# Attention after a group norm: the weighted sum of values by key tile in four PSUM banks, the projections in the banks of the scores

## The reference

```
x:   32 images of 32 x 32 places with 256 channels, float32
n  = group norm of x per image (32 groups of 8 channels, eps 1e-5)
q, k, v = n Wq + bq, n Wk + bk, n Wv + bv          (1024 tokens x 256)
attn    = softmax(q k^T / 16) over the keys
out     = x + (attn v) Wo + bo
```

## Time and profile before

| | us |
|---|---|
| median of three runs (lowest, highest) | 1810.69 (1810.49, 1810.78) |
| the profiled execution, its own time | 1810.44 |
| its span, first to last instruction | 1808.7 |
| PE busy in it | 1800.0 |
| DVE busy | 1662.2 |
| ACT busy | 985.4 |

### The profile page before, as it was taken

The page is one execution under the profiler, slowest core; times in us unless marked ns, Lnnn a source line. Parts: engine busy times, 40 slices in busy tenths (PEclk is TensorE's granted clock), DMA queues, the critical chain, the costliest instruction groups (busy, mean ns, idle before and its releaser), DMA issues.

```text
span 1808.7 us, 32719 instructions
## 1 busy us (share of the span) xinstructions
PE 1800.0 (100%) x11589; PEld 1643.6 (91%) x11589; DVE 1662.2 (92%) x2924; ACT 985.4 (54%) x1352; POOL 91.2 (5%) x106
## 2 busy tenths in 40 slices
PE   9999999999999999999999999999999999999999
PEld 8989999899998998999999989999899898999989
DVE  7999999999999999999999999999999999999997
ACT  4564554655645546556465564554654645646553
POOL 0000000000000000000000000000000000000000
PEclk9999999999999999999999999999999999999999
DMA  3221122221223202223122221122220222212201
GB/s 117 59 70 43 39 70 58 70 62 20 70 58 70 69 13 69 61 66 70 36 46 70 58 70 51 30 70 58 70 67 14 70 58 70 70 22 59 67 14 36
DMA packets 28808, 101.92 MB, mean 56 GB/s; under 512 B 3189, under 2 KB 3962, under 8 KB 28794
## 3 DMA queue, kind: packets, MB, share of 16 engines
q0 software_dynamic: 9072, 33.03, 11.7%
q1 hardware_dynamic: 19722, 68.69, 11.6%
HBM read 68.16 MB, written 66.58 MB: 74 GB/s over the span
## 4 chain that ended last, share of the span: by engine, by line
PE 96%; DVE 2%; issue 1%; ACT 1%; DMA 0%; POOL 0%; SPq 0%; DVEq 0%; POOLq 0%
PE ps_s L832 47%; PE ps_o L920 13%; PE ps_o L922 13%; PE ps_o L921 13%; PE ps_o L832 10%; DVE top L577 0%; DMA s_buf<-in_L_conv_Wk_dram 0%; DVE s_buf L607 0%; ACT s_buf L349 0%; ACT p_hi L343 0%; DVE o_buf L627 0%; DVE bn_parts L482 0%; DVE h_lo L550 0%; POOL group_stats L292 0%; ACT s_buf L335 0%
## 5 line engine op out<-in xcount | busy, mean ns | idle before, releaser
L920 PE MATMUL ps_o<-v_rows,p_hi 128*128 128x258 f32 x2048 | 581.5, 284 | 0.0
L922 PE MATMUL ps_o<-v_rows,p_lo 128*128 128x258 f32 x2048 | 576.4, 281 | 0.0
L921 PE MATMUL ps_o<-v_lo,p_hi 128*128 128x256 f32 x2048 | 574.4, 280 | 0.0
L343 ACT ACTIVATE p_hi<-s_buf 128x1024 fp32r<-128x1024 f32 x256 | 272.0, 1063 | 506.4 <-DVE s_buf L607 506.4
L832 PE MATMUL ps_s<-g_hi,h_hi 128*128 128x512 f32 x1024 | 399.3, 390 | 1.5 <-DVE v_lo L563 1.4
L832 PE MATMUL ps_s<-g_hi,h_lo 128*128 128x512 f32 x1024 | 399.0, 390 | 0.0
L832 PE MATMUL ps_s<-g_lo,h_hi 128*128 128x512 f32 x1024 | 398.8, 389 | 0.0
L921 PEld LDWEIGHTS ps_o<-v_lo,p_hi 128*128 128x128 f32 x2048 | 388.9, 190 | 2.9
L920 PEld LDWEIGHTS ps_o<-v_rows,p_hi 128*128 128x128 f32 x2048 | 385.8, 188 | 2.4
L922 PEld LDWEIGHTS ps_o<-v_rows,p_lo 128*128 128x128 f32 x2048 | 387.4, 189 | 0.0
L335 ACT ACTIVATE s_buf<-ps_s 128x512 f32<-128x512 f32 x512 | 292.8, 606 | 160.3 <-PE ps_s L832 158.8
(11 more groups left out here) (95 smaller groups left out, 2197.3 us busy)
## 6 DMA issues: line engine op xcount, KB each, us to landing
x_t<-in_x_turned_dram SPq DMA_DIRECT2D x64, 512.0 KB, 3.9
out_dram<-in_x_dram SPq DMA_DIRECT2D x63, 512.0 KB, 7.6
out_dram<-o_buf POOLq DMA_DIRECT2D x63, 512.0 KB, 5.5
x_last<-in_x_dram SPq DMA_DIRECT2D x1, 512.0 KB, 8.2
out_dram<-o_buf SPq DMA_DIRECT2D x4, 128.0 KB, 2.1
s_buf<-in_L_conv_Wq_dram SPq DMA_DIRECT2D x1, 256.0 KB, 5.0
s_buf<-in_L_conv_Wk_dram SPq DMA_DIRECT2D x1, 256.0 KB, 5.3
s_buf<-in_L_conv_Wv_dram SPq DMA_DIRECT2D x1, 256.0 KB, 5.5
```

Source lines behind the costliest of these rows:

```text
L343: nc.scalar.activation(p_hi[c][:, rows, :], s_buf[c][:, rows, :], ACT.Exp, scale=SCALE).then_inc(p_hi_done, 1)
L920: nc.tensor.matmul(ps[:, 0:VC], p_hi[c][:, m, cols], v_hi[:, m, :], start=m == 0, stop=False)
L921: nc.tensor.matmul(ps[:, 0:C], p_hi[c][:, m, cols], v_lo[:, m, :], start=False, stop=False)
L922: last = nc.tensor.matmul(ps[:, 0:VC], p_lo[c][:, m, cols], v_hi[:, m, :], start=False, stop=m == T - 1)
```

## The change

The attend loops over the key tiles outside and the four query tiles inside (`weigh`, `keys_ready`, `attend`), so that the four banks of `ps_o` are open at once and a piece of `p_lo` and `v_lo` is waited for when its key tile comes. The last attend of all keeps the old loop order (`attend_last`). The projections of g and v use the four banks of `ps_s`; the constants' banks are swapped in return. `scores` therefore waits for a g or v low part at each of its first four key tiles, and `project_v` for the scores of the chunk before it, bank by bank. DVE gets new orders: in the loop all finishes stand later (finish 0 after the stats, 1 behind project 0, 2 and 3 between the p_rests), and in the last image the four differences and the four finishes of (30, 1) stand ahead of the v_rests. ACT changes in the first image (order of v) and in the last (v parts between the exps). Left out of the diff are the two orders of the first image: there the v_rests stand between part maxima, query maxima, row maxima and the first two differences, in the order 0 to 3, and the four finishes of (0, 0) between the last p_rests of (0, 1).

```
...
         ps_s = banks("ps_s", SB)
         ps_o = banks("ps_o", TQ)
-        ps_g = [ps_o[0], ps_o[1], ps_s[2], ps_s[3]]
-        ps_turn = [ps_o[0], ps_o[1], ps_s[2]]
-        ps_a, ps_vo, ps_gb, ps_ob, ps_idle = ps_s[0], ps_s[1], ps_s[3], ps_o[3], ps_o[2]
+        ps_g = ps_s
+        ps_turn = [ps_s[0], ps_s[1], ps_s[2]]
+        ps_a, ps_vo, ps_gb, ps_ob, ps_idle = ps_o[0], ps_o[1], ps_o[2], ps_o[3], ps_s[3]
         ident = sb("ident", [P, P])
...
-        FIRST_V = (2, 3, 0, 1)
...
                 nc.scalar.activation(g_hi[:, k, c * Q:(c + 1) * Q], ps_g[i][:], ACT.Identity,
                                      bias=g_bias[:, k:k + 1]).then_inc(g_hi_done, 1)
-            def v_part(b, i, nth=None):
-                act.wait_ge(v_ps, b * 4 + (i if nth is None else nth) + 1)
+            def v_part(b, i):
+                act.wait_ge(v_ps, b * 4 + (i + 1))
                 nc.scalar.activation(v_hi[:, 2 * i:2 * i + 2, 0:C], ps_g[i][:].rearrange("p (t n) -> p t n", t=2),
                                      ACT.Copy).then_inc(v_hi_done, 1)
...
                     exponentials(b, 0, i)
                     scores_out(b, 1, 3 + i)
                 scores_out(b, 1, 7)
-                for i in range(4):
-                    v_part(b, i)
-                for i in range(NP):
+                exponentials_hi(b, 1, 0)
+                exponentials(b, 1, 0)
+                v_part(b, 0)
+                v_part(b, 1)
+                exponentials_hi(b, 1, 1)
+                v_part(b, 2)
+                exponentials(b, 1, 1)
+                v_part(b, 3)
+                for i in (2, 3):
                     exponentials_hi(b, 1, i)
                     exponentials(b, 1, i)
...
                                                in1=g_hi[:, k, cols].bitcast(F32), op0=ALU.add,
                                                op1=ALU.subtract).then_inc(g_lo_done, 1)
-            def v_rest(b, i, nth=None):
-                dve.wait_ge(v_hi_done, b * 4 + (i if nth is None else nth) + 1)
+            def v_rest(b, i):
+                dve.wait_ge(v_hi_done, b * 4 + (i + 1))
                 nc.vector.tensor_tensor(v_lo[:, 2 * i:2 * i + 2, :], ps_g[i][:].rearrange("p (t n) -> p t n", t=2),
                                         v_hi[:, 2 * i:2 * i + 2, 0:C].bitcast(F32), ALU.subtract).then_inc(v_lo_done, 1)
...
             def softmax_beside(b, c, finish_tile, h_next, project, next_stats, next_sums):
                 part_maxima(b, c)
-                finish_tile(0)
                 query_maxima(b, c)
-                finish_tile(1)
                 row_maxima(b, c)
                 h_next(0)
                 h_next(1)
                 difference(b, c, 0)
                 difference(b, c, 1)
-                finish_tile(2)
                 difference(b, c, 2)
                 next_stats()
+                finish_tile(0)
                 project(0)
                 next_sums()
-                finish_tile(3)
+                finish_tile(1)
                 project(1)
                 p_rest(b, c, 0)
                 project(2)
                 difference(b, c, 3)
                 project(3)
                 p_rest(b, c, 1)
+                finish_tile(2)
                 p_rest(b, c, 2)
+                finish_tile(3)
                 p_rest(b, c, 3)
             def body(b):
...
                 p_rest(b, 0, 3)
                 for step in range(2, 5):
                     maxima(b, 1, step)
-                finish(b - 1, 1, 0)
                 part_maxima(b, 1)
-                finish(b - 1, 1, 1)
                 query_maxima(b, 1)
-                finish(b - 1, 1, 2)
                 row_maxima(b, 1)
-                finish(b - 1, 1, 3)
-                for i in range(4):
-                    v_rest(b, i)
-                difference(b, 1, 0)
-                difference(b, 1, 1)
+                for i in range(NP):
+                    difference(b, 1, i)
+                for j in range(TQ):
+                    finish(b - 1, 1, j)
+                v_rest(b, 0)
+                v_rest(b, 1)
+                p_rest(b, 1, 0)
+                v_rest(b, 2)
+                p_rest(b, 1, 1)
+                v_rest(b, 3)
+                p_rest(b, 1, 2)
                 finish(b, 0, 0)
-                difference(b, 1, 2)
-                p_rest(b, 1, 0)
-                difference(b, 1, 3)
                 finish(b, 0, 1)
-                p_rest(b, 1, 1)
-                p_rest(b, 1, 2)
+                p_rest(b, 1, 3)
                 finish(b, 0, 2)
-                p_rest(b, 1, 3)
                 finish(b, 0, 3)
                 dve.wait_ge(x_last_in, 16)
                 nc.vector.tensor_tensor(x_last[:], x_last[:], out_bias[:].unsqueeze(1).broadcast_to([P, TQ, C]),
...
                     if first and i == 2:
                         pe.wait_ge(h_hi_done, 2)
                         pe.wait_ge(h_lo_done, 2)
-                    if first and i == 3:
-                        pe.wait_ge(fold_done, 2)
-                    if i < 2:
-                        after(pe, o_out, b * 8 + (i + 1 - 8))
-                    elif i == 2:
+                    if i == 0:
                         after(pe, s_out, b * 16)
                     rows, cols = slice(k * P, (k + 1) * P), slice(c * Q, (c + 1) * Q)
                     product(ps_g[i][:], [(a[:, kk, rows], h[:, kk, cols]) for kk in range(K)
                                              for a, h in ((a_hi, h_hi), (a_hi, h_lo), (a_lo, h_hi))], g_ps)
-            def project_v(b, scores_done=8, first=False):
-                for i in FIRST_V if first else range(4):
-                    if first and i >= 2:
-                        pe.wait_ge(s_out, i + 5)
-                    elif i < 2:
-                        after(pe, o_out, b * 8 + (i + 1 - 4))
-                    elif i == 2:
-                        pe.wait_ge(s_out, b * 16 + scores_done)
+            def project_v(b, scores_done=8):
+                for i in range(4):
+                    pe.wait_ge(s_out, b * 16 + (scores_done - 3 + i))
                     for tt in range(2):
                         cols = slice((2 * i + tt) * P, (2 * i + tt + 1) * P)
                         product(ps_g[i][:, tt * C:(tt + 1) * C],
...
                                  for h, w in ((h_hi, vo_hi), (h_hi, vo_lo), (h_lo, vo_hi))],
                                 v_ps if tt == 1 else None)
-            def scores(b, c, m, ahead_of_v=False, first_v=False):
-                if m == 0:
-                    pe.wait_ge(g_lo_done, b * 4 + (2 * c + 2))
-                if m in (2, 3) and first_v:
-                    pe.wait_ge(v_lo_done, FIRST_V.index(m) + 1)
-                elif m in (2, 3) and not ahead_of_v:
-                    pe.wait_ge(v_lo_done if c else g_lo_done, b * 4 + (m + 1))
+            def scores(b, c, m, ahead_of_v=False):
+                if m < SB and c == 0:
+                    pe.wait_ge(g_lo_done, b * 4 + max(2, m + 1))
+                elif m < SB and not ahead_of_v:
+                    pe.wait_ge(v_lo_done, b * 4 + (m + 1))
                 after(pe, s_out, b * 16 + (8 * c + m + 1 - SB))
                 rows, cols = slice(m * P, (m + 1) * P), slice(c * Q, (c + 1) * Q)
                 product(ps_s[(8 * c + m) % SB][:], [(h[:, kk, rows], g[:, kk, cols]) for kk in range(K)
                                                     for h, g in ((h_hi, g_hi), (h_hi, g_lo), (h_lo, g_hi))], s_ps)
-            def attend(b, c, j, by_piece=False, last_block=False):
-                if j == 0 and not by_piece:
-                    pe.wait_ge(v_lo_done, b * 4 + 4)
-                if j >= 2 or last_block:
-                    after(pe, o_out, b * 8 + (4 * c + j + 1 - 4))
+            def weigh(b, c, m, j):
                 ps, cols = ps_o[j], slice(j * P, (j + 1) * P)
+                nc.tensor.matmul(ps[:, 0:VC], p_hi[c][:, m, cols], v_hi[:, m, :], start=m == 0, stop=False)
+                nc.tensor.matmul(ps[:, 0:C], p_hi[c][:, m, cols], v_lo[:, m, :], start=False, stop=False)
+                last = nc.tensor.matmul(ps[:, 0:VC], p_lo[c][:, m, cols], v_hi[:, m, :], start=False,
+                                        stop=m == T - 1)
+                if m == T - 1:
+                    last.then_inc(o_ps, 1)
+            def keys_ready(b, c, m):
+                if m % PIECE == 0:
+                    pe.wait_ge(p_lo_done, b * 8 + (4 * c + m // PIECE + 1))
+                    pe.wait_ge(v_lo_done, b * 4 + (m // PIECE + 1))
+            def attend(b, c):
                 for m in range(T):
-                    if j == 0 and m % PIECE == 0:
-                        pe.wait_ge(p_lo_done, b * 8 + (4 * c + m // PIECE + 1))
-                        if by_piece:
-                            pe.wait_ge(v_lo_done, b * 4 + (m // PIECE + 1))
-                    nc.tensor.matmul(ps[:, 0:VC], p_hi[c][:, m, cols], v_hi[:, m, :], start=m == 0, stop=False)
```

(62 more changed lines are left out.)

## The result

The changed kernel takes **1817.39 us** (1817.20 to 1818.34), the kernel before in the same comparison 1810.53: a ratio of 1.0039, 95% interval 1.0028 to 1.005. It is slower by 6.86 us, where 3.8 were forecast. The profiled execution took 1818.34 us, 0.95 more than the median.

What follows compares the result with a forecast made beforehand. PE was taken as the bound, busy 1800.0 of 1808.7 us. Last image +4.57, last attend +0.05 and image 1 -0.85, loop and attends 0, sum to +3.77 us: 1814.5 us against the median, range 1811.3 to 1820.5.

Steps and rivals of the forecast that it cites:

- The last image: Last image: v_rests behind four differences and four finishes start attend (31, 0) late, +4.57 us, ends 3.9 and 5.1.
- nothing gives it back: both attends behind it, 192 matmuls, are on PE: Last image: the late start of +4.57 us is not recovered by the two attends that follow on PE.
- the lower clock: Rival, attends: the clock falls to 1.2 GHz there, doubling one 11.44 us attend per image, 2169 us; chance 0.01.
- +0.05 for the last attend: Last attend: it needs finish (31, 0, 0), about 1798.4, where PE wants it at 1798.45; +0.05 us.
- The bank-cycling rule: Attends: a skill rule says cycling PSUM banks can let the clock fall; it speaks against the change, kept as last rival.
- The loop: 28 images: DVE's chain to the second g_lo ends 961.93, no stall and no margin; 0, ends 0 and 0.35 us per image.
- PE wants to start the next scores at 906.37 + 55.80: Loop: PE's wanted start of the next scores is 962.17, against 962.16 when g_lo allows it.
- The rival of the late chain: Rival, loop: DVE's chain to the second g_lo exceeds PE's by 0.05 to 0.35 us per image, 1817.4 us; chance 0.28.
- The 0.15 us of drains: Loop, DVE before the second g_rest: drains that the two dropped finishes hid come back, 0.15 us later.
- Attend spacing and bank changes: Attends: 31 bank changes and twelve waits leave each at 11.44 us; 0, ends -5.4 and +5.7 us in all.
- POOL's power at 2.05 us in every image: Loop: DVE, 0.4 us late, starts the maxima unheld; POOL's power takes 2.05 us, maxima to turn back 2.22 for 1.15.
- Image 1: Image 1: v gives back 0.95 us, scores of image 2 at 124.3 instead of 125.14; -0.85 us, ends 0 and -2.0.

Runs made afterwards that it cites:

- experiment 2: The changed kernel, with the last image's four v_rests all ahead of the differences, p_rests behind, and ACT's v parts ahead of the exponentials: 1811.34 us, ratio 1.0004.
- experiment 4: One tiny DVE reduction added behind the variance: on the changed kernel 1817.69 us (ratio 1.0038), on experiment 1's kernel 1812.36 us (1.0008).
- experiment 7: Experiment 2's kernel with finish 1 of each loop image's second softmax moved behind the second g_rest: 1807.93 us, ratio 0.9987.
- experiments 7 and 8: 8 is three controls: experiment 7 with finish 0 moved too, 1809.08 us; experiment 6 with finish 1 moved, 1810.67; the kernel before with finish 3 moved, 1810.25.
- experiment 5: Three tiny DVE reductions added behind the variance: on the changed kernel 1820.15 us (ratio 1.0054), on experiment 2's kernel 1813.19 us (1.0015).
- experiment 3: As experiment 1, but with two of the last image's four differences ahead of the v_rests: 1814.69 us, ratio 1.0019.
- experiment 1: The changed kernel with the last image's old order: finishes and first two v_rests ahead of the differences, ACT's v parts ahead of the exponentials: 1812.41 us, ratio 1.0009.
- experiment 6: Experiment 2's kernel with the attend looping over query tiles outside again, DVE orders and g and v banks kept: 1813.06 us, ratio 1.0013.

## Why the prediction was right, and where its sizes were off

**The last image: right, with a term missing.** +4.57 was forecast and V to A grew by 4.49; experiment 2 took it back. The step that failed is "nothing gives it back: both attends behind it, 192 matmuls, are on PE", which took them at their old length. Behind 4.3 us of idle time they ran slower: +2.19 us in the profiled execution, 24.37 - 22.83 = +1.54 in that of the first kernel of experiment 4, whose last image is the same. I had put the lower clock at a chance of 0.01, and in the wrong place. Of the +0.05 for the last attend nothing shows: PE waits for nothing there.

**The bank-cycling rule.** In experiment 7 every attend but the last cycles its four banks, PE is busy in all of the 28 images and the granted clock is 1.00; the attends of the kernel after take 11.446 us, before 11.442. The Trainium skill (TensorE: Matmul & The Clock Gate, "A second HAM failure mode: psum-queue depth-cycling") describes a case in which such cycling makes the clock swing; the traces here don't agree for this kernel. In the traces here the clock fell only where PE had been idle.

**The loop: a right chain, a wrong conclusion at its edge.** Brought to the same start of V, the steps hold: first v_rest forecast at 931.37, measured 931.37; last p_rest 940.31 and 940.30; turn back 946.3 and 946.25; the second `g_lo` 961.62 and 961.66. The step that failed is the other side of the comparison, "PE wants to start the next scores at 906.37 + 55.80". PE is quicker behind an attend by key tile: G by 0.044 us, the scores of chunk 1 by 0.016, V by 0.008, against 0.004 more in each of the two attends; 55.733 against 55.793 for the image without a stall (experiments 7 and 8). I took 0 for it, with the attend's own length as the only place to look. So PE came 0.06 us earlier to a chain that had 0.01 us of margin. The stall cost 55.854 - 55.733 = 0.12 us an image, of which 0.06 were given back by the shorter stages. The difference, 28 x 0.06 = 1.7 us less 0.07 in the first image behind image 1, is the +1.62 of the table. The rival of the late chain was right, and its price per image of 0.1 was near for the stall, though not for the net. The 0.15 us of drains in that sum has no row of its own; the sum as a whole came out 0.04 us short.

**Attend spacing and bank changes: 0 forecast, +0.004 us an attend measured,** 0.25 us in 63. **POOL's power at 2.05 us in every image: right**, 107.21 - 78.69 = 28.5 us more of it, 1.02 in each of 28. **Image 1:** -0.85 forecast, about -0.5 measured. The `v_lo` wait fell from 1.4 to 0.5 as forecast; `h_lo` stayed at 1.0; the g low parts came 0.44 us earlier where 0.84 was forecast. The steps between were not tested alone. **Start, stores, loads: 0**, and nothing in the runs speaks against it.

**The total.** -0.5 for image 1, +1.6 for the loop, +4.5 for the gap and about +1.2 for the clock make 6.8; 6.86 was measured. The 1.2 is an estimate: 2.19 less the 0.95 by which the profiled execution was over the median. It takes the low clock to be the whole of that 0.95, which fits the mean clocks (0.999 in the three executions up to 1817.39, 0.998 in the two above) but was not shown by a trace.

**Luck in the number.** The forecast was 3.8 and the excess of 3.1 us is 1.6 of the loop, 1.2 of the clock and 0.3 of image 1. The range held it because of the room left for the late chain; over a third of the excess came from the clock instead, a term with a chance of 0.01. That the rival of the late chain said 1817.4 is a coincidence: it had 2.9 us for the loop, where 1.6 were measured.

## What to carry to other kernels

When the bounding engine is 100% busy by the table, compare stage lengths by start to start at 0.01 us: a late operand that costs 0.1 us per image is in no wait of PE, only in the row of its weight loads, and moving one 0.6 us operation behind the one that is waited for was worth 3.4 us here. Price a gap on PE at more than its length when it is some microseconds long: here the matmuls behind 4.3 us of it ran at half the clock for 1.5 to 2.2 us more, and 1.9 us were not safely short. And where a chain comes out with no margin, take the stall and not the zero: both sides of the comparison move with the change.

## What the runs showed of the hardware

- An idle PE and the clock: a gap of 4.3 us brought the granted clock to 0.50 and cost 2.19, 1.54 and 2.07 us in three profiled executions (after, and experiments 4 and 5 on it). A gap of 1.9 us left it at 1.00 in the one profiled execution of experiment 3, and one of 1.99 us near the start of the same execution was followed by 0.50 from 9.12 us on; the mean clocks of that kernel's other executions speak for a fall in most. A gap of 0.9 us (experiment 1) left it at 1.00, its attends being longer by 23.93 - 22.83 = 1.10 us, the wait and a little more.
- POOL against DVE. In each long case POOL's power ends 0.89 us behind the end of DVE's two-input operation: 946.15 and 945.26 in after, 945.82 and 944.93 in experiment 4, 947.13 and 946.24 in experiment 5. So it waits for DVE's end, also where its record starts 0.02 us ahead (experiment 5); in the kernel before, 0.05 us ahead (943.29 against 943.34), it took 1.03 us. The Trainium skill (SBUF — State Buffer, "🔬 SBUF: two separate sides") has the pair of ports locked by whoever comes first; the traces agree, if coming first is not read from the starts in the record, which lie ahead of it.
- The matmuls of a projection of g behind a query-outer attend stand 0.231 us apart for the first ten, behind a key-tile attend 0.227. That the loop order does it is shown by experiment 6; why is open.
